# Queries and keys in two fp16 parts, two heads side by side in the row halves of TensorE, in a two-block transformer kernel

## What is computed

```python
xn = _layernorm(x)
x = x + attn0(xn) + ffn0(xn)     # 16 heads of 16, ALiBi, causal, softmax clamped at 1e-10; 8 gated experts
xn = _layernorm(x)
x = x + attn1(xn) + ffn1(xn)     # 16 heads of 16, causal softmax; ternary weights, gelu, output rounded to 4 bits
# scores of a head, in both blocks:
scores = einsum('bhqd,bhkd->bhqk', q, k) * 16 ** -0.5
```

## Time and profile before

| | |
|---|---|
| median of 3 runs | 858.34 us (857.8 to 860.27) |
| the profiled execution | 856.29 us, span 854.6 us |
| busy: TensorE, VectorE, ScalarE, GpSimd | 80%, 72%, 69%, 21% of the span |
| mean granted TensorE clock | 0.918 of full speed |
| HBM read, written | 42.10 MB, 30.93 MB |

### The profile page before, as it was taken

The page is one execution under the profiler, slowest core; times in us unless marked ns, Lnnn a source line. Parts: engine busy times, 40 slices in busy tenths (PEclk is TensorE's granted clock), DMA queues, the critical chain, the costliest instruction groups (busy, mean ns, idle before and its releaser), DMA issues.

```text
span 854.6 us, 19350 instructions
## 1 busy us (share of the span) xinstructions
PE 684.0 (80%) x5856; PEld 539.7 (63%) x5856; DVE 614.7 (72%) x2239; ACT 588.4 (69%) x1753; POOL 178.2 (21%) x205
## 2 busy tenths in 40 slices
PE   0686544889878997989798997899798978897756
PEld 0464433668756785868676875688576856685533
DVE  3978746887677876787688767787678776766364
ACT  2455421887759794888488775979498848966764
POOL 6011021132113211131113211321113111320222
PEclk9889876999989998999989997999899999998975
DMA  6752005040413123130504040312313050300661
GB/s 194 267 148 87 1 1 160 2 148 16 128 48 111 37 79 108 40 109 13 174 1 148 13 145 30 111 37 87 100 57 91 13 160 2 124 26 1 191 202 52
DMA packets 55195, 73.94 MB, mean 87 GB/s; under 512 B 4544, under 2 KB 47680, under 8 KB 55104
## 3 DMA queue, kind: packets, MB, share of 16 engines
q1 hardware_dynamic: 52064, 69.22, 26.2%
q0 software_dynamic: 1056, 2.62, 1.0%
q10 hardware_dynamic: 1984, 1.21, 0.5%
HBM read 42.10 MB, written 30.93 MB: 85 GB/s over the span
## 4 chain that ended last, share of the span: by engine, by line
PE 39%; ACT 19%; DVE 18%; issue 15%; DMA 6%; ACTq 1%; SPq 1%; DVEq 1%; POOL 1%; POOLq 0%
PE gen_ps L972 9%; PE gen_ps L983 6%; ACT probs L875 5%; PE value_ps L1056 4%; PE gen_ps L1015 4%; DVE probs L1321 3%; PE gen_ps L946 3%; DVE probs L1332 3%; PE gen_ps L1003 3%; ACT hid L859 3%; ACT pt L884 3%; PE turn_ps L1033 2%; PE gen_ps L958 2%; PE turn_ps L1035 2%; PE turn_ps L1034 2%
## 5 line engine op out<-in xcount | busy, mean ns | idle before, releaser
L875 ACT ACTIVATE probs<-probs,nmax 128x256 f32<-128x256 f32 (+1 forms) x512 | 227.3, 447 | 57.1 <-DVE nmax L1321 55.8
L1321 DVE CUSTOM_DVE_ANT_0 probs<-score_ps,bias 128x256 f32<-128x256 f32 (+1 forms) x512 | 158.6, 352 | 62.8 <-PE score_ps L1027 60.1
L744 POOL TENSOR_TENSOR h_lo<-hid,h_hi 128x512 f16<-128x512 f32 x64 | 76.0, 1187 | 419.6 <-ACT h_hi L852 405.1
L884 ACT ACTIVATE pt<-turn_ps 128x384 f32<-128x384 f32 x256 | 121.4, 477 | 38.5 <-PE turn_ps L1035 38.5
L972 PE MATMUL gen_ps<-xe_hi,gu_hi 128*128 128x256 f16 x512 | 103.8, 287 | 5.2 <-DVE v_sb L1192 4.6
L972 PE MATMUL gen_ps<-xe_lo,gu_hi 128*128 128x256 f16 x512 | 103.7, 286 | 0.0
L972 PE MATMUL gen_ps<-xe_hi,gu_lo 128*128 128x256 f16 x512 | 103.5, 286 | 0.0
L875 ACT ACTIVATION_READ_ACCUMULATOR probs<-probs,nmax 128x1 f32 x512 | 97.4, 190 | 0.0
L1026 PE MATMUL score_ps<-k_stack,q_stack 96*128 96x256 bf16 x256 | 72.9, 287 | 28.8 <-DMA k_stack<-scr_k 15.2
L1033 PE MATMUL turn_ps<-ident,probs 128*128 128x128 f32 x256 | 76.7, 299 | 21.0 <-DVE probs L1332 15.7
L1332 DVE TENSOR_SCALAR probs<-probs,rsum 128x256 f32<-128x256 f32 (+1 forms) x256 | 87.5, 384 | 4.6
(11 more groups left out here) (169 smaller groups left out, 1530.0 us busy)
## 6 DMA issues: line engine op xcount, KB each, us to landing
q_stack<-scr_q SPq DMA_DIRECT2D x32, 384.0 KB, 3.9
k_stack<-scr_k SPq DMA_DIRECT2D x32, 384.0 KB, 5.1
scr_q<-parts SPq DMA_DIRECT2D x16, 384.0 KB, 2.7
scr_k<-parts SPq DMA_DIRECT2D x16, 384.0 KB, 3.3
scr_q<-parts SPq DMA_DIRECT2D x16, 256.0 KB, 3.6
scr_k<-parts SPq DMA_DIRECT2D x16, 256.0 KB, 3.6
x<-in_x SPq DMA_DIRECT2D x8, 256.0 KB, 3.0
scr_q<-parts SPq DMA_DIRECT2D x16, 128.0 KB, 2.9
```

Of the source, the lines that this page charges most:

```text
L744: pool.tensor_tensor(h0_lo[:, e], hid0[:, e], h0_hi[:, e], ALU.subtract).then_inc(s_h0l, 1)
L875: last = act.activation(probs[:, k, lo:hi], probs[:, k, lo:hi], ACT.Exp, scale=-1.0, bias=nmax[:, k, j:j + 1], accum_out=total)
L884: act.activation(pt[:, slot:slot + 3].rearrange("p t q -> p (t q)"), turn_ps[s % 2][:, 0:3 * P], ACT.Copy).then_inc(s_ev, 1)
L1321: last = dve.tensor_tensor_reduce(out=probs[:, k, lo:hi], in0=g[:, lo:hi], in1=bias[:, blo:S], scale=-1.0, scalar=BIG, op0=ALU.add, op1=AL ...
```

## The change

Queries and keys go into two fp16 parts instead of three bf16 parts, and all four products are taken, not six. A head's stack is 4 x 16 = 64 rows, so that two heads stand in one stack, the even one in rows 0 to 63, the odd one in rows 64 to 127. At an even head TensorE runs four matmuls: 256 columns for each of the two heads, then 128 for each; at an odd head none. Before them it waits until VectorE is done with both banks, that is, with head s-1. The steps `r` and `m` go, and `l` writes the second part. SP issues four stores instead of six, and four loads a stack instead of two. The reciprocals of block 1 are taken of one number per head and query (`inv1`, 16 columns) and then copied to the 256 columns of `rsum1`, with a wait between. The host permutes the channels so that a pair's heads land in the two halves.

The rest keeps steps of one kind in rising order (`in_turn`), works out the places of `down` in the sum from the list, and adds waits on VectorE for results that are ready already (before `gated`, and before the first `down`). `turn`, `value` and the strings' remaining order are as before.

```diff
-SPLITS = 6
+SPLITS = 4
-LAG = {"scalar": {"score": 4, "m1": 1, "up": 4, ...
+LAG = {"scalar": {"score": 4, "up": 4, ...
...
-        parts = sb("parts", [P, 2, 3, 2, S], BF16)
-        q_stack = [sb(f"q_stack{i}", [KR, H // 2, S], BF16) for i in range(2)]
+        parts = sb("parts", [P, 2, 2, 2, S], F16)
+        q_stack = [sb(f"q_stack{i}", [2 * KR, H // 4, S], F16) for i in range(2)]
...
             def store_parts(l, n):
                 wait(sp, s_pl[l], n.at(1, 1))
-                for a, (lo, hi) in enumerate(((0, 3), (3, 5), (5, 6))):
-                    sp.dma_start(scr[l][0][lo:hi].rearrange("s (p m) n -> p s (m n)", p=P),
-                                 flat[:, 0, 0:hi - lo]).then_inc(s_scr[l], 16)
-                    sp.dma_start(scr[l][1][lo:hi].rearrange("s (p m) n -> p s (m n)", p=P),
-                                 flat[:, 1, a:a + 1].broadcast_to([P, hi - lo, 2 * S])).then_inc(s_scr[l], 16)
+                for a in range(2):
+                    sp.dma_start(scr[l][0][2 * a:2 * a + 2].rearrange("s (p m) n -> p s (m n)", p=P),
+                                 flat[:, 0, a:a + 1].broadcast_to([P, 2, 2 * S])).then_inc(s_scr[l], 16)
+                    sp.dma_start(scr[l][1][2 * a:2 * a + 2].rearrange("s (p m) n -> p s (m n)", p=P),
+                                 flat[:, 1]).then_inc(s_scr[l], 16)
...
-                half = slice(8 * (u % 2), 8 * (u % 2) + 8)
-                for src, dst in zip(scr[l], (q_stack, k_stack)):
-                    sp.dma_start(dst[u % 2][:], src.rearrange("s (c h) n -> (s c) h n", h=H)[:, half, :])\
-                      .then_inc(s_stack[u % 2], 16)
+                for hp in range(2):
+                    four = slice(8 * (u % 2) + 4 * hp, 8 * (u % 2) + 4 * hp + 4)
+                    for src, dst in zip(scr[l], (q_stack, k_stack)):
+                        sp.dma_start(dst[u % 2][KR * hp:KR * hp + KR],
+                                     src.rearrange("s (c h) n -> (s c) h n", h=H)[:, four, :]).then_inc(s_stack[u % 2], 16)
...
-                if name in ("m0", "m1"):
-                    l = int(name[1])
-                    wait(act, s_pr[l], n.at(1, 1))
-                    act.activation(parts[:, :, 1], rest[:], ACT.Copy).then_inc(s_pm[l], 1)
...
                 if name == "score":
                     s = st.arg
-                    u, hh = s // 8, s % 8
-                    if hh == 0:
-                        wait(pe, s_stack[u % 2], st.it.at(64, 32 * (u // 2)))
-                    wait(pe, s_mx, heads_before(st, -1))
-                    g, q, k = score_ps[s % 2], q_stack[u % 2], k_stack[u % 2]
-                    pe.matmul(g[:, 0:S], q[:, hh, P:S], k[:, hh, :], start=True, stop=True)
-                    pe.matmul(g[:, S:S + P], q[:, hh, 0:P], k[:, hh, 0:P], start=True, stop=True).then_inc(s_sc, 1)
+                    if s % 2:
+                        return
+                    u, i = s // 8, s % 8 // 2
+                    if i == 0:
+                        wait(pe, s_stack[u % 2], st.it.at(128, 64 * (u // 2)))
+                    wait(pe, s_mx, heads_before(st))
+                    rows = [slice(KR * hp, KR * hp + KR) for hp in range(2)]
+                    q, k = q_stack[u % 2], k_stack[u % 2]
+                    for hp in range(2):
+                        pe.matmul(score_ps[hp][:, 0:S], q[rows[hp], i, P:S], k[rows[hp], i, :], start=True, stop=True)
+                    for hp in range(2):
+                        pe.matmul(score_ps[hp][:, S:S + P], q[rows[hp], i, 0:P], k[rows[hp], i, 0:P],
+                                  start=True, stop=True).then_inc(s_sc, 1)
...
-                if name in ("r0", "r1"):
+                if name in ("l0", "l1"):
                     l = int(name[1])
                     wait(dve, s_ph[l], n.at(6, 6))
-                    dve.tensor_tensor(rest[:], rest[:], parts[:, :, 0], ALU.subtract).then_inc(s_pr[l], 1)
-                if name in ("l0", "l1"):
-                    l = int(name[1])
-                    wait(dve, s_pm[l], n.at(1, 1))
-                    dve.tensor_tensor(parts[:, :, 2], rest[:], parts[:, :, 1], ALU.subtract).then_inc(s_pl[l], 1)
+                    dve.tensor_tensor(parts[:, :, 1], rest[:], parts[:, :, 0], ALU.subtract).then_inc(s_pl[l], 1)
...
                 if name == "norm" and head_block(st) == 1 and st.arg % 8 == 7:
                     wait(dve, s_ex, heads_before(st, 1))
+                    dve.reciprocal(inv1[:], esum1[:, st.arg % H // 8]).then_inc(s_iv, 1)
                     wait(dve, s_pv, st.it.at(2 * H // G4, (st.arg - 7) // G4 - H // G4))
-                    dve.reciprocal(rsum1[:].rearrange("p t h c -> p (t h) c"),
-                                   esum1[:, st.arg % H // 8].rearrange("p t h -> p (t h)").unsqueeze(2)
-                                   .broadcast_to([P, NT * H // 2, C])).then_inc(s_rr, 1)
+                    wait(dve, s_iv, batch_of(st, 1).at(2, st.arg % H // 8 + 1))
+                    dve.tensor_copy(rsum1[:].rearrange("p t h c -> p (t h) c"),
+                                    inv1[:].unsqueeze(2).broadcast_to([P, NT * H // 2, C])).then_inc(s_rr, 1)
```

More of the change, by code:

```diff
@@ L75, with in_turn @@
 TURNED = 8
-LAG = {"scalar": {"score": 4, "m1": 1, "up": 4, "q0": 1, "turn": 1, "up:1": 5, "value:1": 0, "turn:4": 0},
[1 row of a table removed]
+LAG = {"scalar": {"score": 4, "up": 4, "q0": 1, "turn": 1, "up:1": 5, "value:1": 0, "turn:4": 0},
+       "vector": {"gate": 1, "up": 1, "down": 2, "op0": 2, "w2": 8, "l1": 2, "qmax": 8, "norm": 2,
                   "gate:3": 2, "gate:7": 2, "gate:6": 0, "score:0": 1, "norm:1": 4, "score:18": 2, "gate:5": 2,
                   "score:9": 2, "norm:9": 4, "up:0": 0, "score:3": 1}}
+def in_turn(items, key):
+    turns = {}
+    for item in items:
+        turns.setdefault(key(item)[0], []).append(item)
+    turns = {name: iter(same if name == "setup" else sorted(same, key=key)) for name, same in turns.items()}
+    return [next(turns[key(item)[0]]) for item in items]
 def with_heads(order, last):
@@ L138 @@
 """
-BLOCK1 = {"ln1a", "ln1b", "tr1", "q1", "k1", "r1", "m1", "l1", "v1", "w1", "h1", "w2", "op1", "qmax", "quant", "fetch"}
+BLOCK1 = {"ln1a", "ln1b", "tr1", "q1", "k1", "l1", "v1", "w1", "h1", "w2", "op1", "qmax", "quant", "fetch"}
 def order_of(text, last):
@@ L150, in order_of @@
             out.append((name, int(arg or 0), int(word.startswith("+")) - int(name in BLOCK1)))
-    return with_heads(out, last)
+    steps = iter(in_turn([x for x in out if not isinstance(x, int)], lambda x: (x[0], x[2], x[1])))
+    return with_heads([x if isinstance(x, int) else next(steps) for x in out], last)
 SPLIT = [("qk", 0), ("gu", 0), ("wd", 0), ("gu", 1), ("gu", 2), ("wd", 2), ("gu", 3), ("gu", 4), ("wd", 4), ("gu", 5),
@@ L210, in stages @@
         users = last_users(kind, it)
-    out, place, after_down = [], 0, {}
+    out = []
+    places = {step[0:2]: i for i, step in enumerate(x for x in ORDERS[kind] if x[0] in ("down", "op0"))}
     use = USES_BEFORE[kind]
@@ L220, in stages @@
         if st.name == "up":
-            st.place = after_down.get(st.arg - 2, 0)
+            st.place = places.get(("down", st.arg - 2), -1) + 1
         if st.name in ("down", "op0"):
[L223 to L226, removed]
+            st.place = places[st.name, st.arg]
         out.append(st)
     late = [i + lag.get(f"{st.name}:{st.arg}", lag.get(st.name, 0)) for i, st in enumerate(out)]
-    return [out[i] for i in sorted(range(len(out)), key=lambda i: (late[i], i))]
+    return in_turn([out[i] for i in sorted(range(len(out)), key=lambda i: (late[i], i))],
+                   lambda st: (st.name, st.n.off, st.arg))
 def last_users(kind, it):
@@ L659, in _ @@
                 do(st)
-            for counts, batch in ((s_yw, 16), (s_x2w, 16), (s_scr[1], 96)):
+            for counts, batch in ((s_yw, 16), (s_x2w, 16), (s_scr[1], 64)):
                 sp.sem_inc(counts, batch)
@@ L1379, in by_channel @@
     def by_channel(w):
-        w = w.reshape(-1, H, C).transpose(0, 2, 1)
+        heads = [8 * u + 2 * i + hp for u in range(2) for hp in range(2) for i in range(4)]
+        w = w.reshape(-1, H, C)[:, heads].transpose(0, 2, 1)
         return w.reshape(-1, P, 2).transpose(0, 2, 1).reshape(-1, H * C)
```

41 lines of the change are left out of this document (21 added, 20 removed), and 1 row of the table LAG.

## The result

The changed kernel takes 869.76 us (median of 4 runs, 868.76 to 871.32) against 858.47 us of the kernel before beside it: a ratio of 1.013 (95% interval 1.0108 to 1.0152). It is slower by 11.3 us; 5.4 us faster was predicted, and 869.8 lies outside the range of 843 to 865.

The account below looks back on a forecast made before the run. No compute engine is full; a chain of waits that changes engine within each loop body was taken as the bound. Terms +5.4 - 4.6 - 1.0 - 3.0 - 2.2 = -5.4 us gave 852.9 us, range 843 to 865.

Parts of the forecast that it names:

- the wait for head s-1: In each loop body, TensorE's pairs at heads 14 and 16 wait for VectorE: +1.9 us a body.
- there VectorE holds the chain, ... and they hide: First pass: waits at four heads are hidden and cost nothing; without that cover, 6 us in all.
- The pair: Two heads' scores on TensorE take 0.34 us, no gain and no loss; ends 0.17 and 0.68 us.
- Rival 1: Dividing the array costs its drain, x more per pair, 63 pairs: 874.3 us at x = 0.34; chance 0.20.
- Rival 2: The array's halves work side by side and waits shrink; pairs of 0.17 us give 842.2 us; chance 0.22.
- Steps r and m: In each body, m0 leaving ScalarE brings -1.0 us; r1 and m1 bring nothing in the loop.
- Stores and loads of the parts: In the first batch and before the loop, fewer stores and shorter landings: -2.3 us each, -4.6 us together.
- third rival: Landings do not change: loads keep their time, x2's store stays behind them; +7.6 us, 860.5 us; chance 0.16.
- The end: Last batch: m1 off the chain, -1.0 us, and x2's store landing sooner, -3.0 us.
- the reciprocals: Block 1 on VectorE: short reciprocal and copy save 1.1 us each; two of sixteen on the chain, -2.2 us.

Follow-up runs that it names:

- e7: The changed kernel with 18 redundant matmuls while TensorE waits at head 14 and 5 at head 16: 859.37 us.
- e9: e6 with two heads issued together over the full array after the wait for head s-1: 865.05 us.
- e6: The changed kernel with one head at a time over 96 rows, 32 of them zeros, and the wait for head s-2: 844.24 us.
- e1: The kernel before, with only the wait ahead of an even head changed, to head s-1 instead of s-2: 885.73 us.
- e3: The kernel before, with only block 1's reciprocals changed to 16 columns and a copy to 256: 856.44 us.
- e4: The kernel before, with the scores' matmuls over 64 of the stacks' 96 rows: 878.66 us.
- e5_moved: The changed kernel with the pairs of heads 14 and 16 moved later on TensorE's queue: 849.47 us.

## Why the prediction was wrong

**The price of the wait for head s-1 is the step that failed**, by two things that it left out. The place was right: both pairs wait where they were said to, 2.64 and 0.64 us. Where the clock stays up, the size was right too: 1.88 us against +1.9 a body, the turn of head 11 1.35 to 1.5 us late against 1.5, and e7 shows it in all six bodies. But 11 us were carried for the wait in the whole kernel, and e9 less e6 is 20.8.

The first omission is TensorE's clock behind the wait: 1.5 us in each of four bodies and 2.9 in the first, 8.9 us in all. I took the durations of the matmuls behind the wait from a trace in which TensorE had not stood there. Its rows had the lower price as well: the same twelve matmuls take 2.56 us at 430.10 and 1.31 us at 464.39.

The second is "there VectorE holds the chain, ... and they hide". In the first pass of the changed kernel TensorE waits for VectorE at four pairs, 3.09, 2.43, 3.29 and 1.66 us (waits by releaser ahead of 152 us: us, times, longest):

```profile
PE score_ps L1036 <- DVE nmax L1331: 10.5, 4, 3.3
```

These waits are not hidden in full. The first `turn` of the first body starts at 148.3 us in e6 and at 151.6 in e9, 3.3 us later; e1 is 2.5 us behind the kernel before there. Two executions that are alike up to there can differ by about 1 us (before and e3 by 1.3), so the size is rough, but it is not zero; the prediction's other end was 6 us. In the two profiled executions e9 less e6 is then 3.3 us ahead of the loop, 11.3 for the wait and 9.6 for the clock in the six bodies, and a little less than nothing elsewhere, 23.4 in all.

**The pair: right in the net, for half of a reason.** 0.34 us was taken and 0.42 measured. Ends of 0.17 and 0.68 held it. Rival 1 had x = 0.34 at most and decided from 0.09 on; x is 0.08, and by e9 some 3 to 5 us in all. This is enough to undo most of the forecast's gain and not enough to make the kernel 11 us slower, so the rival's time, 874.3, is near the measured one by another cause. The price behind it, 0.24 us for a head that enters the divided array alone, is shown by e4 and is larger than the 0.09 that I could see into `value`. The Trainium skill, "TensorEngine Tiling (Array Packing)", Key Properties, says that a change of mode drains TensorE, and that tiles run independently; the runs agree with both, 0.24 us lost and two matmuls in one's time.

**Rival 2** (halves side by side, waits shrink) had its first half: they overlap. The waits did not shrink, they grew. Its 0.17 us for a pair left out the price of the division, 0.24 us.

**Steps r and m.** Set side by side, e6 is 1.0 us ahead of the kernel before behind the place of m0, as predicted, but 0.7 of it are given back at the start of the next body, where TensorE waits 4.67 us for VectorE's rows instead of 3.96. Five bodies together gain 2.4 us and not 5; what VectorE is late by there was not tried.

**Stores and loads of the parts.** -4.6 us was predicted ahead of the loop. Nearly all of it came: e6 reaches the first `turn` of the first body 3.6 us sooner than the kernel before. The changed kernel keeps only 1.3 of this, since the first pass's waits and the pairs' price take the rest. In the first batch the stack lands 2.5 us sooner, but behind the wait of 3.09 us at the third pair, at 55.96, the changed kernel is already 1.6 us behind e6 (at 59.48). The third rival's mechanism (the landings do not change) does not hold: the last load that the chain goes through at the loop's entry takes 3.59 us instead of 5.10, and x2's landing is shorter as well.

**The end.** Predicted -1.0 - 3.0 - 2.2 = -6.2 us, measured -5.8 in the changed kernel: x2's landing -3.9, the reciprocals larger than predicted; the pairs' waits in the last passes take some of it back (behind 730 us TensorE waits for VectorE's scores 21 us in the changed kernel, which is not what they cost). The landing takes 2.2 to 3.8 us in all profiled executions with four stores of the parts and 4.3 to 6.1 us in those with six, so 6.08 was the upper end of what it takes before.

**The sum by the runs.** 859 us, less 15 for all that the change removes (e6; the prediction had 16.8), plus 20.8 for the wait (e9), plus 4.7 for the division less the overlap, gives 869.8. That it closes is no proof, since each step is the difference of neighbouring runs. What speaks for the sizes are runs outside this chain: e5_moved takes 20.3 us off by moving two pairs, e7 takes 10.4 us off by keeping the clock up, and e1 puts 26 us on the kernel before.

## What to carry to other kernels

An operand with fewer rows than its neighbours is not always free: here short matmuls of 64 rows between matmuls of 128 cost 0.24 us a head, and filling the stack with zeros up to 96 rows took that away. Dividing the array may still pay where much work runs in one division in a row; no run here tried it. Before two independent steps are fused into one issue, look at what stands behind the later one's wait on that engine, and give the sum a second value in which the work behind the new stop runs at the lower clock. "It hides" is a term of the sum too: give it a price until a row shows the cover. If a fusion must stay, moving its two or three waiting places on the queue can take back what it costs (20 us here).

## What the runs showed of the hardware

A head of 64 rows alone among matmuls of 128 rows costs 0.24 us more than one of 96 rows: 0.09 going in, 0.10 in itself, 0.05 coming out (e4). Two row halves work side by side at no extra time for the second: the pair keeps TensorE 0.27 us, as one head of 64 rows does. After 2.65 us of standing TensorE was granted 1.2 GHz for five to eleven groups of matmuls in five of six bodies of the changed kernel, and full clock in the sixth; in e1 it fell in two of six. With the standing time filled by work whose result nobody uses, the clock stayed up in all six and the kernel was 10.4 us faster (e7). What makes the difference between the bodies is open.
